# Idle products left out before the experts and before the recurrence; expert rows queued ahead of weights, early sums queued later

## The chip, the core and the metric

The kernel runs on one core of one Trainium2 chip. The metric is the device time of one execution in microseconds (us). TensorE is called PE here, VectorE DVE, ScalarE ACT, GpSimd POOL and SyncE SP. SP computes nothing; its queue issues most of the DMAs. All numbers in the text are in us unless another unit stands beside them.

## What is computed

Two transformer-like blocks follow each other on 1024 rows of 256 numbers. A layernorm stands behind each of the four parts.

```python
x = _layernorm(x + attention(x))            # 16 heads, causal, low-rank keys and values
x = _layernorm(x + experts64(x))            # 64 experts, 8 per row, room for 128 rows in each
x = _layernorm(x + recurrence(x))           # gated recurrence over the sequence and a gated branch
x = _layernorm(x + experts8(x))             # 8 experts, 2 per row, and a shared expert

# experts64
topw, topi = jax.lax.top_k(probs, 8); topw = topw / jnp.sum(topw, axis=-1, keepdims=True)
xe = jnp.zeros((64, 128, 256)).at[flat_e, pos].set(x_rep, mode='drop')
g, u = jnp.split(jnp.einsum('ech,ehf->ecf', xe, gate_up_proj), 2, axis=-1)
ye = jnp.einsum('eci,eih->ech', jax.nn.silu(g) * u, down_proj)
y = jnp.sum(y_flat.reshape(-1, 8, 256) * topw.reshape(-1, 8)[..., None], axis=1)

# recurrence
f = jnp.tanh(x @ w_f); g = jax.nn.sigmoid(x @ w_i) * jax.nn.silu(x @ w_v)
state = ft * state + gt                     # scan over the 1024 rows
out = jax.nn.silu((x @ w_q) * states) @ w_ro + ((x @ w_up) * jax.nn.silu(x @ w_gate)) @ w_down
```

## The kernel before, in words

Each engine has a program of its own, written out by hand. The order in the code is the order on the engine, and semaphores tie the engines together. The 1024 rows are 8 tiles of 128. Three stretches matter here.

**Tail of the routing.** Rows go to the experts through a buffer in memory, `xe_d`. POOL's `send` (L658) issues 8 indirect DMAs for each tile, one for each of a row's 8 choices. The choices are sorted, so that choice k of a row never goes to an expert below k. For the last tile this comes after the attention: `transpose_x1`, `route` and `count_places` on PE, the choosing on DVE, then the 8 sends. Behind `count_places` PE runs 40 products that nobody reads (`run_idle`, L1584), and 6 ahead of `transpose_x1`. SP loads the rows of experts two at a time (`load_rows`, L504), experts 0 and 1 when sends 0 and 1 of the last tile have landed, 2 and 3 behind sends 2 and 3, and so on to 7. Then SP issues `w_c` and `wo_c` (L524 and L525), 2 MB of weights of the recurrence, and only then the loop that loads rows and weights of experts 8 and up. The weights of experts 0 to 7 are loaded at the end of the attention.

**The 64 experts.** A ring of 8 buffers holds rows (`xe`) and weights (`gu_w`, `dn_w`). For each expert PE transposes the rows (`transpose_rows`, L1786, called T here), multiplies with the first weights (`gate_up`, L1797) and with the second (`down`, L1807). PE's order is T(e+2), gate_up(e+1), down(e). DVE copies, multiplies and works out where each row goes home to (`find_mine`, `find_home`), ACT does the silu and scales the result, and POOL sends 128 result rows home (`send_home`, L688). Experts 0 to 7 and 56 to 63 are written out; the 48 between them run as a hardware loop of 6 turns on PE, DVE and ACT. T(10) opens the first turn, and T(58) is the first behind the loop.

**The gap and the recurrence.** When all results are home, SP gathers the 8 results of each row (`load_results`, L536), the first four choices in one load, the others in a second. PE meanwhile runs 58 more unread products, in parts that wait for `moved` and `gath`. POOL adds choices 0 and 1 onto 2 and 3 (`sum_early`, L702). DVE adds the rest (`combine`, L1294), L1076 to L1080 take the variance, POOL makes `rstd` (L653), DVE normalises to `x2` (`finish_x2`, L1084), PE transposes (`transpose_x2`, L1830) and projects (`project`, L1840, in three parts). DVE's `middle` multiplies the gates (L1314), scans (L1317), and closes with L1320 and L1325. POOL's order within step t is `rstd` of tile t+1, `sum_early(t+2)`, `rstd` and normalising of tile t-1 (L708). DVE's order in step t is combine(t+1), the adding of the mix of t-1 (L1332), finish_x2(t+1), variance of the mix, middle(t). During this stage SP also loads 1 MB of `w1` for the last part with each tile (L516).

Of the kernel before, what the change touches and what calls it, by code (L numbers as in the profile page):

```python
# [7 lines left out]
T, HID = 1024, 256  # L8
TILES = T // P
# [22 lines left out]
KEY = T * E0  # L32
IDLE_START = 10
# [3 lines left out]
def build(nc, x, xT, wq, wq_ropeT, wkv_aT, kv_ln, wkv_b, woT, router0T, gate_up0, down0, w_in, init_state,  # L37
# [5 lines left out]
    with ctx:  # L43
# [116 lines left out]
        w_c = cutC2(6, HC, HID)  # L160
        wo_c = cutC2(2, HC, HID)
# [101 lines left out]
        sent_last = moved[1::2]  # L263
# [8 lines left out]
        gath_early = [sem(f"gath_early{u}") for u in range(2)]  # L272
        early_summed, sum_step = sem("early_summed"), sem("sum_step")
# [35 lines left out]
        def home_turn(e, u):  # L309

            return turn(e, u) + (32 if u % 2 else 0)
# [136 lines left out]
        def _(sp):  # L448
# [69 lines left out]

            for u in range(2):
# [29 lines left out]
            for t in range(TILES):  # L549
# [50 lines left out]
        def _(pool):  # L600
# [54 lines left out]
            def send(t, k):  # L655
# [3 lines left out]
                                        None).then_inc(sent[k % 2] if t < TILES - 1 else sent_last[k // 2], 16)  # L659
# [32 lines left out]
            for e in range(RING):  # L692
                send_home(e, e)
            with pool.Fori(1, E0 // RING) as i:
                for u in range(RING):
                    send_home(RING * i + u, u)
# [45 lines left out]
        def _(act):  # L742
# [93 lines left out]
            for e in range(RING):  # L836
                expert_act(e + 1, (e + 1) % RING)
                expert_out(e, e)
            with act.Fori(1, E0 // RING - 1) as i:
                for u in range(RING):  # L840
                    expert_act(RING * i + u + 1, (u + 1) % RING)
# [1219 lines left out]
```

## Time and profile before

| | us |
|---|---|
| three runs | 835.5, 831.17, 835.47 |
| their median | 835.47 |
| the profiled execution | 835.53 |
| its span in the trace | 833.7 |

The profiled execution is 1.8 longer than its span, which is what lies around the first and the last instruction. PE is busy for 94% of the span, DVE for 68%, ACT for 48% and POOL for 33%. The busy time of PE holds the unread products too. A row of a timeline reads: start, duration, engine, line, operation, output and inputs, count, and in brackets the idle time ahead of it with what ended it. Merged rows (x8 and the like) span from the first start to the last end.

### The profile page before, as it was taken

How to read it: one execution, taken by the hardware profiler on the slowest of the kernel's cores; microseconds unless marked ns; L12 is line 12 of the kernel's file. 1: busy time of each engine (PE TensorE's matmuls, PEld its weight loads, DVE VectorE, ACT ScalarE, POOL GpSimd, SP SyncE). 2: the span in 40 equal slices, each digit the busy share in tenths (PEclk: the TensorE clock that was granted, in tenths of full speed). 3: DMA queues.
4: the chain of work that ended last, by engine and by line, in shares of the span. 5: the costliest groups of instructions: out<-in, count | busy, mean ns of one | idle time of the engine just before them, and what ended most of it. 6: DMA issues, size and time to landing. Idle time of an engine off the chain costs nothing.

```text
span 833.7 us, 16672 instructions
## 1 busy us (share of the span) xinstructions
PE 780.8 (94%) x4645; PEld 662.9 (80%) x4645; DVE 565.5 (68%) x1422; ACT 397.6 (48%) x898; POOL 272.0 (33%) x357
## 2 busy tenths in 40 slices
PE   7999989999999999999897999998889999999997
PEld 6888867778778777777697898897888778888786
DVE  5323778777877777777644677458857367777766
ACT  1325656655566666666323444312333256666531
POOL 2004445443343333230354565614422500000061
PEclk9998999999999999999998999999998999999999
DMA  7449961000000000000559999777720335555431
GB/s 210 105 104 370 405 238 41 28 28 28 28 21 28 21 18 24 14 28 15 167 157 342 355 357 360 260 254 251 304 102 20 107 112 151 153 151 151 120 94 65
DMA packets 63032, 120.63 MB, mean 145 GB/s; under 512 B 18304, under 2 KB 31616, under 8 KB 62848
## 3 DMA queue, kind: packets, MB, share of 16 engines
q1 hardware_dynamic: 51984, 95.41, 34.9%
q0 software_dynamic: 7680, 21.51, 7.2%
q10 hardware_dynamic: 3312, 3.02, 1.0%
q8 instruction: 29, 0.48, 0.2%
q14 instruction: 27, 0.22, 0.1%
HBM read 76.13 MB, written 43.78 MB: 144 GB/s over the span
## 4 chain that ended last, share of the span: by engine, by line
PE 69%; DVE 12%; issue 7%; ACT 4%; DMA 3%; POOL 3%; SPq 1%; DVEq 0%; ACTq 0%; POOLq 0%
PE scores L1578 9%; PE scores L1577 9%; PE scores L1576 9%; PE probsT_ps L1687 6%; PE scores L1797 5%; PE acc_ps L1987 5%; PE acc_ps L1714 4%; PE misc_ps L1702 4%; PE misc_ps L1700 3%; DVE xT_lo L1054 2%; PE misc_ps L1584 2%; DVE neg_max L1048 2%; PE scores L1807 2%; POOL xd_d L729 2%; PE scores L1840 2%
## 5 line engine op out<-in xcount | busy, mean ns | idle before, releaser
L778 ACT ACTIVATE area<-scores,neg_max 128x128 f32<-128x128 f32 (+7 forms) x128 | 94.9, 742 | 76.7 <-DVE neg_max L1048 75.7
L1048 DVE TENSOR_REDUCE neg_max<-scores 128x1 f32<-128x128 f32 (+7 forms) x128 | 95.7, 749 | 24.6 <-PE scores L1663 24.5
L1687 PE MATMUL probsT_ps<-ident,area 128*128 128x128 f32 x552 | 84.1, 277 | 12.9 <-DVE xT_lo L1054 12.0
L1054 DVE TENSOR_TENSOR xT_lo<-probsT_ps,xT_hi 128x512 fp32r<-128x512 f32 x92 | 62.9, 687 | 38.3 <-ACT xT_hi L785 36.7
L1687 PEld LDWEIGHTS probsT_ps<-ident,area 128*128 128x128 f32 x552 | 63.1, 143 | 24.9 <-issue 19.5
L658 POOL DMA_INDIRECT xe_d<-x_rows,send_i x64 | 64.1, 1001 | 55.8 <-ACT x_rows L802 38.8
L688 POOL DMA_INDIRECT ye_d<-area,home_i x64 | 61.4, 959 | 48.9 <-issue 23.0
L1797 PE MATMUL scores<-area 128*96 128x128 f32 x512 | 68.7, 278 | 1.1 <-DVE area L1220 0.6
L1576 PE MATMUL scores<-kT_hi,weff_hi 128*128 128x512 f32 (+3 forms) x172 | 67.1, 390 | 1.9 <-issue 1.3
L785 ACT ACTIVATE xT_hi<-probsT_ps 128x512 fp32r<-128x512 f32 x92 | 54.0, 594 | 25.1 <-PE probsT_ps L1687 24.8
L1797 PEld LDWEIGHTS scores<-area 128*96 128x96 f32 x512 | 60.5, 166 | 3.2 <-DVE area L1220 2.5
L1578 PE MATMUL scores<-kT_hi,weff_lo 128*128 128x512 f32 (+3 forms) x172 | 62.1, 361 | 0.0
L646 POOL CAST weff_hi<-area 128x256 fp32r<-128x256 f32 x42 | 17.0, 406 | 137.8 <-PE scores L1663 90.2
L1577 PE MATMUL scores<-kT_lo,weff_hi 128*128 128x512 f32 (+3 forms) x172 | 62.0, 360 | 0.0
L1714 PE MATMUL acc_ps<-area,sgd 128*128 128x256 f32 x196 | 60.2, 389 | 1.6 <-DVE x_rows L1071 1.2
L735 POOL DMA_INDIRECT area<-yd_d,slot x16 | 15.8, 984 | 137.4 <-DMA yd_d<-area 132.8
L1702 PE MATMUL misc_ps<-xT_lo,xT_hi 128*128 128x512 f32 x144 | 57.8, 402 | 0.7 <-DVE xT_lo L1054 0.6
L1700 PE MATMUL misc_ps<-xT_hi 128*128 128x512 f32 x96 | 47.7, 497 | 0.0
L1576 PE MATMUL scores<-xT_hi,weff_hi 128*128 128x512 f32 x110 | 46.0, 419 | 0.0
L826 ACT ACTIVATE area<-scores 96x128 f32<-96x128 f32 x64 | 17.5, 273 | 57.1 <-PE scores L1797 57.1
L1987 PE MATMUL acc_ps<-area 128*128 128x256 f32 x184 | 43.5, 379 | 0.8 <-DVE area L1462 0.8
L1071 DVE SCALAR_TENSOR_TENSOR x_rows<-acc_ps,rinv,x_rows 128x256 f32<-128x256 f32 x90 | 42.3, 470 | 2.2 <-PE acc_ps L1714 2.2
(258 smaller groups left out, 1944.5 us busy)
## 6 DMA issues: line engine op xcount, KB each, us to landing
area<-gate_up SPq DMA_DIRECT2D x32, 384.0 KB
area<-w SPq DMA_DIRECT2D x23, 512.0 KB, 3.9
xe_d<-area SPq DMA_DIRECT2D x8, 1088.0 KB, 11.3
area<-xe_d SPq DMA_DIRECT2D x32, 272.0 KB, 6.2
ye_d<-area SPq DMA_DIRECT2D x8, 1024.0 KB, 16.7
area<-ye_d SPq DMA_DIRECT2D x16, 512.0 KB, 4.9
area<-w SPq DMA_DIRECT2D x8, 1024.0 KB, 7.3
area<-down SPq DMA_DIRECT2D x32, 192.0 KB
```

The lines of the kernel that those rows point to most:

```text
L778: act.activation(row_of(n)[:, 0:L], score_bank(n)[:, 0:L], ACT.Exp, bias=neg_max[:, n % 4:n % 4 + 1], accum_out=rsum[:, s, k:k + 1]).then_ ...
L1048: dve.tensor_reduce(neg_max[:, n % 4:n % 4 + 1], score_bank(n)[:, 0:(n // HEADS + 1) * P], AX.X, ALU.max, negate=True).then_inc(max_ready, 1)
L1054: dve.tensor_tensor(pT_lo[b % 3], seat_of("block", b)[:], pT_hi[b % 3].bitcast(f32), ALU.subtract).then_inc(lo_done, 1)
L1576: pe.matmul(out_ap, lh, rh, start=start, stop=False)
L1577: pe.matmul(out_ap, lh, rl, start=False, stop=False)
L1578: return pe.matmul(out_ap, ll, rh, start=False, stop=stop)
L1687: last = pe.transpose(seat_of("block", b)[:, i * P:(i + 1) * P], row_of(QUAD * G + i)[:, k * P:(k + 1) * P], ident[:])
L1700: pe.matmul(ctx_ps[:], latent[:, k, :], pT_hi[b % 3], start=k == 0, stop=False)
L1702: pe.matmul(ctx_ps[:], latent[:, k, :], pT_lo[b % 3], start=False, stop=k == tile_of(G)).then_inc(ctx_step, 1)
L1714: pe.matmul(out_of(n), ctxT[:, G % 2, i * P:(i + 1) * P], wvo[:, h * HID:(h + 1) * HID], start=True, stop=True).then_inc(out_ready, 1)
L1797: last = pe.matmul(half[b][0:I0, part * P:(part + 1) * P], gu_w[:, u, c, part * I0:(part + 1) * I0], xeT[:, b, c, :], start=c == 0, stop=c ...
L1987: last = pe.matmul(acc[:, 0:HID], hdT[:, u, c * P:(c + 1) * P], w2_b[:, u, c, :], start=c == 0, stop=c == I1 // P - 1)
```

## The change

- PE's `run_idle` calls between the attention and the recurrence are gone: 6 and 40 products in the tail of the routing, 58 in the gap. The 10 at the very start stay.
- The weights of experts 0 to 15 (`IN_ADVANCE = 16`) are loaded in 8 DMAs into `area1`, which held the queries of the attention, as soon as POOL has split the last queries. `w_c` and `wo_c` follow them there.
- SP loads the rows of expert 0 behind send 0 and those of expert 1 behind send 1. Rows of experts 8 and 9 follow those of 6 and 7 directly. The ring of weights serves experts 16 and up.
- The first two experts' parts of `w1` now share their place with `w_c` and `wo_c`, so they are loaded after the recurrence.
- PE, DVE, ACT and POOL have the 64 experts written out; SP keeps its loop for experts 24 and up.
- POOL waits for `x2` of tile t+1 ahead of `sum_early(t+2)`.

```diff
+IN_ADVANCE = 16
-        sent_last = moved[1::2]
+        sent_last = moved[0:2] + [moved[k | 1] for k in range(2, TOP0)]
+        ld_first_row = sem("ld_first_row")
...
-                if past(e, RING):
+                if past(e, IN_ADVANCE + RING):
                     sp.wait_ge(ye_ps, e + 2 - RING)
...
-            sp.wait_ge(pT_ps, blocks_to(GROUPS))
-            for e in range(0, RING, 2):
-                load_weights(e, e)
-            sp.wait_ge(x1_done, TILES)
+            sp.wait_ge(q_split, TILES * PAIRS)
+            for e in range(0, IN_ADVANCE, 4):
+                sp.dma_start(first_gu[:, e:e + 4], gate_up0[:, e:e + 4]).then_inc(ld_first, 16)
+                sp.dma_start(first_dn[:, e:e + 4, :], down0[:, e:e + 4, :]).then_inc(ld_first, 16)
+            sp.dma_start(w_c, w_in).then_inc(ld_wc, 16)
+            sp.dma_start(wo_c, w_mix).then_inc(ld_wc, 16)
...
-            for e in range(0, RING, 2):
-                sp.wait_ge(sent_last[e // 2], 32)
+            for e in range(2):
+                sp.wait_ge(sent_last[e], 16)
+                sp.dma_start(xe[:, e:e + 1, :], xe_v[:, e:e + 1]).then_inc((ld_first_row, ld_xe[0])[e], 16)
+            for e in range(2, RING, 2):
+                sp.wait_ge(sent_last[e], 32)
                 load_rows(e, e)
-            sp.dma_start(w_c, w_in).then_inc(ld_wc, 16)
-            sp.dma_start(wo_c, w_mix).then_inc(ld_wc, 16)
-            with sp.Fori(1, E0 // RING) as i:
+            for e in range(RING, IN_ADVANCE + RING, 2):
+                load_rows(e, e % RING)
+                if e < 2 * RING:
+                    load_weights(IN_ADVANCE + e - RING, e % RING)
+            with sp.Fori(1 + IN_ADVANCE // RING, E0 // RING) as i:
...
-                load_w1(t)
+                if t + 2 < E1:
+                    load_w1(t + 2)
             sp.wait_ge(x3_done, TILES)
+            load_w1(0)
+            load_w1(1)
...
                 if before(t, TILES - 2):
+                    pool.wait_ge(x2_done, t + 2)
                     sum_early(t + 2, u)
...
-            for e in range(RING):
-                transpose_rows(e + 2, (e + 2) % RING)
-                gate_up(e + 1, (e + 1) % RING)
-                down(e, e)
-            with pe.Fori(1, E0 // RING - 1) as i:
...
-            for e in range(E0 - RING, E0):
+            for e in range(E0):
                 if e + 2 < E0:
                     transpose_rows(e + 2, (e + 2) % RING)
...
-            run_idle(8)
-            for u in range(RING - 4, RING):
-                pe.wait_ge(moved[u], home_turn(E0 - RING + u, u))
-                run_idle(5)
-            run_idle(10)
-            pe.wait_ge(gath[0], 16)
-            run_idle(20)
```

PE, from the last product of the routing (`count_places`) to the first expert, before:

```order
L1739 MATMUL scores<-chosen,earlier 128x64
L1584 MATMUL misc_ps<-ident 128x128 x14
L1584 MATMUL misc_ps<-ident 128x128 [waits last_sends,send_done]
L1584 MATMUL misc_ps<-ident 128x128 x5
L1584 MATMUL misc_ps<-ident 128x128 [waits last_sends]
L1584 MATMUL misc_ps<-ident 128x128 x19
L1786 MATMUL probsT_ps<-ident,area 128x128 [waits ld_xe0]
```

and in the changed kernel, where L1748 is `count_places` and L1791 is T:

```order
L1748 MATMUL scores<-chosen,earlier 128x64
L1791 MATMUL probsT_ps<-ident,area 128x128 [waits ld_first_row]
L1791 MATMUL probsT_ps<-ident,area 128x128
L1791 MATMUL probsT_ps<-ident,area 128x128 [waits ld_xe0]
L1791 MATMUL probsT_ps<-ident,area 128x128
L1802 MATMUL scores<-area 96x128 [waits ld_first,xeT_done]
```

The 40 unread products are gone, and T(0) waits for its own rows alone.

SP's queue, from the rows of experts 0 to 7 to those of expert 8 (the first L504 row behind the branch), before; `moved1`, `moved3`, `moved5` and `moved7` are the sends of the last tile in pairs:

```order
L504 DMA area<-xe_d 128x544 [waits moved1,sent0_1,sent0_0]
L504 DMA area<-xe_d 128x544 [waits moved3]
L504 DMA area<-xe_d 128x544 [waits moved5]
L504 DMA area<-xe_d 128x544 [waits moved7]
L524 DMA area<-w_in 128x3072
L525 DMA area<-w_mix 128x1024
L526 UNCONDITIONAL_BRANCH
L526 ISA
L504 ISA [waits home_done,xeT_ps]
L504 DMA area<-xe_d 128x544
```

and in the changed kernel, where L545 and L523 load rows and L515 and L516 weights, here of experts 16 and 17:

```order
L545 DMA area<-xe_d 128x272 [waits sent0_1,moved0,sent0_0,pT_ps]
L545 DMA area<-xe_d 128x272 [waits moved1]
L523 DMA area<-xe_d 128x544 [waits moved3]
L523 DMA area<-xe_d 128x544 [waits moved5]
L523 DMA area<-xe_d 128x544 [waits moved7]
L523 DMA area<-xe_d 128x544 [waits home_done,xeT_ps]
L515 DMA area<-gate_up 128x768
L516 DMA area<-down 96x512
```

The 2 MB of `w_in` and `w_mix` no longer stand between the rows of expert 7 and those of expert 8.

POOL in steps 0 and 1 of the recurrence, before (L653 is `rstd`, L702 `sum_early`, L708 the normalising of the tile before):

```order
L653 TENSOR_TENSOR rstd<-mv,minus_half 128x1 [waits var_done] x2
L702 TENSOR_TENSOR area<-area 128x512 [waits gath_early0]
L653 TENSOR_TENSOR rstd<-mv,minus_half 128x1 [waits var_done]
L702 TENSOR_TENSOR area<-area 128x512 [waits gath_early1]
L653 TENSOR_TENSOR rstd<-mv,minus_half 128x1 [waits var_done]
L708 TENSOR_SCALAR x_rows<-y,mv,rstd 128x256 [waits rstd_done]
```

and in the changed kernel, where the three lines are L683, L729 and L735:

```order
L683 TENSOR_TENSOR rstd<-mv,minus_half 128x1 [waits var_done] x2
L729 TENSOR_TENSOR area<-area 128x512 [waits gath_early0,x2_done]
L683 TENSOR_TENSOR rstd<-mv,minus_half 128x1 [waits var_done]
L729 TENSOR_TENSOR area<-area 128x512 [waits gath_early1,x2_done]
L683 TENSOR_TENSOR rstd<-mv,minus_half 128x1 [waits var_done]
L735 TENSOR_SCALAR x_rows<-y,mv,rstd 128x256 [waits rstd_done]
```

Nothing changes places on POOL's queue; `sum_early` gets a second wait, and the `rstd` and the normalising behind it wait with it.

## Rows read from the trace of the kernel before

**Rows 1.** Chain of waits, 360 to 640: start, duration, what.

```profile
428.58 3.50 DMA xe_d<-x_rows,send_i
434.81 9.35 DMA area<-xe_d
542.56 10.31 PE misc_ps L1584 x90
581.67 1.35 DVE area L1084
```

**Rows 2.** Timeline of PE: L1584 unread products, L1786 T of an expert.

```profile
417.91 10.80 PE L1584 MATMUL misc_ps<-ident 128*128 128x128 f32 x80
436.67 0.38 PE L1786 MATMUL probsT_ps<-ident,area 128*128 128x128 f32 x2
444.20 0.69 PE L1786 MATMUL probsT_ps<-ident,area 128*128 128x128 f32 x2 [4.31 <-DMA area<-xe_d]
449.64 0.38 PE L1786 MATMUL probsT_ps<-ident,area 128*128 128x128 f32 x2
525.40 0.38 PE L1786 MATMUL probsT_ps<-ident,area 128*128 128x128 f32 x2
533.10 0.38 PE L1786 MATMUL probsT_ps<-ident,area 128*128 128x128 f32 x2
```

**Rows 3.** Timelines of POOL and SP, and SP's line L504 alone.

```profile
419.64 1.04 POOL L658 DMA_INDIRECT xe_d<-x_rows,send_i  x1 [5.08 <-DVE send_i L1147]
423.50 8.91 SPq L504 DMA_DIRECT2D area<-xe_d  x4
432.46 1.45 SPq L524 DMA_DIRECT2D area<-w_in  x1
DMA to landing us min/median/max: 2.8/6.2/10.4
```

**Rows 4.** Busy time by stretch; behind POOL: granted clock, DMA share, GB/s.

```profile
418.00:419.00 1.00, 1.00 (x9) 1.00 (x8) 0.90 (x6) 0.65 (x3) 0.00 (x0) 0.65 0.01 1
...
421.00:422.00 1.00, 1.00 (x8) 1.00 (x8) 0.00 (x0) 0.00 (x0) 0.95 (x1) 0.65 0.37 139
...
442.00:443.00 1.00, 0.00 (x0) 0.00 (x0) 0.00 (x0) 0.00 (x0) 0.28 (x1) 0.59 1.05 418
...
449.00:450.00 1.00, 1.00 (x9) 0.90 (x9) 0.29 (x2) 0.43 (x2) 0.80 (x1) 0.99 1.09 378
...
480.00:500.00 20.00, 19.86 (x155) 18.18 (x154) 14.36 (x64) 9.47 (x26) 12.27 (x13) 1.00 1.05 358
```

**Rows 5.** The page's DMA issues: count, KB each.

```profile
area<-gate_up SPq DMA_DIRECT2D x32, 384.0 KB
...
area<-down SPq DMA_DIRECT2D x32, 192.0 KB
```

**Rows 6.** Timelines of DVE and PE at the start of the recurrence.

```profile
551.22 0.41 DVE L1084 TENSOR_SCALAR area<-area,mv,rstd 128x256 f32<-128x256 f32 x1 [0.68 <-POOL rstd L653]
...
552.71 0.38 PE L1830 MATMUL misc_ps<-ident,area 128*128 128x128 f32 x2
553.56 3.84 PE L1840 MATMUL scores<-area 128*128 128x128 f32 x32 [0.46 <-ACT area L849]
```

**Rows 7.** Timelines of POOL and DVE in step 4, then at 23.

```profile
581.60 1.27 POOL L702 TENSOR_TENSOR area<-area 128x512 f32<-128x512 f32 x1
...
583.83 0.43 DVE L1314 SCALAR_TENSOR_TENSOR area<-area 128x256 f32<-128x256 f32 x1
583.95 0.71 POOL L653 TENSOR_TENSOR rstd<-mv,minus_half 128x1 f32<-128x1 f32 x1 [1.08 <-DVE mv L1080]
584.29 1.00 DVE L1317 TENSOR_TENSOR_SCAN area<-area 128x128 f32<-128x128 f32 x2
585.75 0.42 DVE L1325 TENSOR_TENSOR area<-area,probsT_ps 128x256 f32<-128x256 f32 x1
...
23.16 0.74 POOL L648 TENSOR_TENSOR q_lo<-area,q_hi 128x256 fp32r<-128x256 f32 x1
23.26 0.92 DVE L1006 TENSOR_TENSOR weff_lo<-area,weff_hi 128x256 fp32r<-128x256 f32 x1
```

More of the change, by code:

```diff
@@ L309, in home_turn, with weights_of, await_weights @@
         def home_turn(e, u):
-            return turn(e, u) + (32 if u % 2 else 0)
+            return turn(e, u) + (16 if u < 2 else 32 if u % 2 else 0)
+        def weights_of(e):
+            if e < IN_ADVANCE:
+                return first_gu[:, e], first_dn[:, e, :]
+            return gu_w[:, e % RING], dn_w[:, e % RING, :]
+        def await_weights(eng, e):
+            if e < IN_ADVANCE:
+                eng.wait_ge(ld_first, 8 * IN_ADVANCE)
+            else:
+                eng.wait_ge(ld_gu[e % RING // 2], 2 * turn(e - IN_ADVANCE, e % RING))
         def steps_two(eng, body):
@@ L691, in _ @@
             pool.wait_ge(zeroed, 16 * ZEROINGS)
-            for e in range(RING):
[L693 to L696, printed above, removed]
+            for e in range(E0):
+                send_home(e, e % RING)
             def sum_early(t, u):
@@ L835, in _ @@
             expert_act(0, 0)
[L836 to L841, printed above, removed]
-                    expert_out(RING * i + u, u)
-            for e in range(E0 - RING, E0):
+            for e in range(E0):
                 if e + 1 < E0:
@@ L1228, in find_mine @@
             def find_mine(e, u):
+                if isinstance(e, int) and e == 0:
+                    dve.wait_ge(ld_first_row, 16)
                 dve.wait_ge(ld_xe[u // 2], turn(e, u))
@@ L1260, in _ @@
             gated(0, 0)
-            for e in range(RING):
-                copy_xeT(e + 2, (e + 2) % RING)
-                gated(e + 1, (e + 1) % RING)
-                if e % 2 == 0:
-                    find_mine(e + 2, (e + 2) % RING)
-                else:
-                    find_home(e + 1, (e + 1) % RING)
-            with dve.Fori(1, E0 // RING - 1) as i:
-                for u in range(RING):
-                    copy_xeT(RING * i + u + 2, (u + 2) % RING)
-                    gated(RING * i + u + 1, (u + 1) % RING)
-                    if u % 2 == 0:
-                        find_mine(RING * i + u + 2, (u + 2) % RING)
-                    else:
-                        find_home(RING * i + u + 1, (u + 1) % RING)
-            for e in range(E0 - RING, E0):
+            for e in range(E0):
                 if e + 2 < E0:
@@ L1772, in _ @@
             count_places(TILES - 1)
-            run_idle(14)
-            pe.wait_ge(send_done, TILES)
-            for j in range(2):
-                pe.wait_ge(last_sends, j + 1)
-                run_idle(6)
-            run_idle(14)
             def transpose_rows(e, u):
-                pe.wait_ge(ld_xe[u // 2], turn(e, u))
+                if isinstance(e, int) and e == 0:
+                    pe.wait_ge(ld_first_row, 16)
+                else:
+                    pe.wait_ge(ld_xe[u // 2], turn(e, u))
                 if past(e, 2):
@@ L1797, in gate_up @@
                         last = pe.matmul(half[b][0:I0, part * P:(part + 1) * P],
-                                         gu_w[:, u, c, part * I0:(part + 1) * I0], xeT[:, b, c, :],
+                                         weights_of(e)[0][:, c, part * I0:(part + 1) * I0], xeT[:, b, c, :],
                                          start=c == 0, stop=c == HC - 1)
@@ L1806, in down @@
                     pe.wait_ge(ye_done, e - 1)
-                pe.matmul(half[2 + b][:, 0:HID], hT[:, b, :], dn_w[:, u, :], start=True, stop=True).then_inc(ye_ps, 1)
+                pe.matmul(half[2 + b][:, 0:HID], hT[:, b, :], weights_of(e)[1], start=True, stop=True).then_inc(ye_ps, 1)
             transpose_rows(0, 0)
@@ L1811, in _ @@
             gate_up(0, 0)
[L1812 to L1821 removed]
+            for e in range(E0):
                 if e + 2 < E0:
```

20 lines of the change are left out of this document (9 added, 11 removed).

## The prediction, made before the changed kernel ran

> **What bounds the kernel now.** I read the chain of waits first, then the timelines of PE, POOL and SP around its long pieces, and last the granted clock by stretches of one us. The chain crosses three places that the change touches [rows 1]: sends and loads of rows with no work in them, unread products just ahead of the recurrence, and a DVE instruction in each step of the recurrence that takes 1.35 where its like takes 0.41 [rows 6].
>
> In the tail of the routing the unread products run from 417.91 to 428.71 [rows 2]. They cost little by themselves: the last tile's first send starts at 419.64, SP loads the first rows at 423.50 [rows 3], and PE could have started some 3 earlier, but would soon have waited, since the last pair of rows is issued only when send 7 has landed, at 428.58 + 3.50 = 432.1 [rows 1]. The loss is later. T(8) starts at 444.20 after 4.31 of waiting for its rows [rows 2], because those stand behind 2 MB of weights on SP's queue [rows 3]. In that wait the granted clock falls (a mean of 0.59 over 442 to 443, so at 442.4 if it goes from full to half at once) and it is back only at 449.0 [rows 4]. Half is 1.2 GHz, full 2.4. T(10) comes at 449.64 instead of about 443.
>
> From T(10) to T(58) the experts take (525.40 - 449.64)/48 = 1.578 each, and in the written-out part from T(58) to T(63) (533.10 - 525.40)/5 = 1.540 [rows 2]. PE sets both paces; it is busy for 19.86 of 20 [rows 4].
>
> In the recurrence DVE sets the step. POOL's early sum starts at 581.60 and ends at 582.87; DVE's L1084 starts at 581.67 and ends at 583.02 [rows 1, 7]. It stands still while POOL works, and PE waits for what it writes.
>
> **The change part by part**, against the profiled execution's own 835.53, which is 0.06 from the median of the three runs; I treat the two as one.
>
> *Tail, up to T(6).* Sends land 2.5 to 3.5 after their issue: for sends 0 and 1, about 423.50 - 420.99, since sends start 1.27 apart from 419.64 [rows 3]. Send 0 has then landed at 422.2, and the least landing time of such a load is 2.8 [rows 3], so T(0) can start at 425.0 and T(1) at 426.3. The rows of 2 and 3 come at about 428.9, of 4 and 5 at 431.4, of 6 and 7 at 432.1 + 2.8 = 434.9. Without the unread products PE has been idle for 7 and starts at half clock, where an expert costs twice 1.525, or 3.05. (1.525 is 1.540 less the small gaps in it.) The clock comes back 3.4 to 4.8 after work begins: it was low from 418.35 to 421.65 while products ran back to back, and T(8) started at 444.20 and the clock rose at 449.0 [rows 2, 4]. With it back at 430 to 433.5, T(6) starts between 436.0 and 437.3; before, it is 436.67 [rows 2]. The three products of `route` and `count_places` may meet a low clock too, for 0 to 0.7. Earlier rows and colder products cancel: **+0.2**, between -0.7 and +1.3.
>
> *T(6) to T(10).* The rows of 8 and 9 now follow at once those of 6 and 7. Their ring places are free (T(1) and `find_home` of 0 are over by 428), so they are issued at 432.6 and land at about 436; T(8) needs them at 440. The early weights, 16 x 288 KB [rows 5] and 2 MB more, are 6.8 MB or 19 at 358 GB/s [rows 4]. They start when POOL has split the last queries, ahead of the last tile's attention, and are in before the last sends. If they were not, the sends would share the DMA engines with them, for a few tenths. Four experts at 1.54 are 6.2 instead of 449.64 - 436.67 = 12.97 [rows 2]: **-6.8**, between -6.8 and -4.3 (if only the wait goes and the clock still falls). What is late next is nothing on DMA: SP's rows of 10 and 11 want T(3), which is over before the rows of 8 have landed.
>
> *Experts written out.* 48 x (1.578 - 1.540) = **-1.8**. The cover is that PE gets its code and weights in time. Two experts' loads and results are 384 + 192 + 272 KB and 2 x 128 KB (the first two from [rows 5], the others from the shapes), 1,104 KB or 1,130,000 bytes; in 2 x 1.540 that is 367 GB/s, against 358 seen with the DMA engines full [rows 4]. If 358 were the ceiling, the loads would fall behind by 0.04 an expert, 1.6 in the 40 that load both rows and weights. A row load lands in 6.2 at the median, and is issued about 7 experts or 10.7 ahead of its use, so some 4 are in hand [rows 3] and PE would not notice. I take the whole, with 0 as the other end.
>
> *The gap.* `x2` of tile 0 is ready at 551.22 + 0.41 = 551.63, yet its transposes start at 552.71, behind the last unread products, which end at 552.87 [rows 1, 6]. That wait goes: -1.0. In exchange PE comes out of 14 idle at half clock. The work up to the end of parts 0 and 1 of `project` is 0.44 + 3.6, and DVE waits for it [rows 6]. With the clock back after 4.8, of which 0.5 is waiting for ACT, half of 4.3 is lost: +2.1. With 3.4 it is +1.4, and if all of it runs at half clock +4.0. Together **+1.1**, between +0.4 and +3.
>
> *Early sums behind x2.* L1084 goes from 1.35 to 0.41 in six tiles. The first is hidden behind PE's cold start, so 5 x 0.94 = 4.7 at most. But POOL's 1.27 now begins at the end of L1084. With X for that end, POOL works from X + 0.1 to X + 1.35, and DVE's L1314, a product of two SBUF tensors, starts at X + 0.8 (583.83 against 583.02) [rows 7]. What that costs is seen at 23: DVE's L1006, also with two SBUF inputs and 0.43 long by itself (its like is L1314 [rows 7]), starts 0.10 behind a POOL instruction that ends at 23.90 and ends itself at 24.18, 0.28 later [rows 7]. So L1314 ends at X + 1.63 instead of X + 1.24, a loss of 0.39, and L1294 behind it may lose 0.05 to POOL's later normalising. L1325 was ready on both sides, PE's and DVE's, so it moves with DVE. 0.94 - 0.44 = 0.5 in 5 steps: **-2.5**, between 0 and -4.7.
>
> The Trainium skill (SBUF — State Buffer, section "Who interferes with whom") says that a DVE instruction with two SBUF inputs contends with a GpSimd one that reads SBUF, and that whoever starts first blocks the other for its whole length. The rows at 23 agree. Taken to the letter it holds for the scans as well.
>
> *The rest.* `w1` parts 0 and 1 are loaded after the recurrence; 2 MB at 358 GB/s is 6, and their first reader stands behind the routing of the last part and half of its shared expert, which is the cover. If that cover were gone, they would cost up to those 6.
>
> The sum: 0.2 - 6.8 - 1.8 + 1.1 - 2.5 = -9.8. **835.5 - 9.8 = 825.7.**
>
> **The rivals.**
>
> *Cold start of the experts.* With gaps between the first rows the clock stays at half until T(6). Four experts from 428.9 at 3.05 put it at 441.1 instead of 436.9: +4.2, or 830. For it: PE has a hole ahead of each of the first loads. Against: once T(2) is in, half-clock work of 3.05 an expert is longer than the 2.5 between two sends that bring two, so PE has no holes. The Trainium skill (TensorE: Matmul & The Clock Gate, section "HAM oscillation — how this bites in real kernels") warns of waits for DMA between bursts of products, each of which begins at half clock again; it speaks against taking the unread products out.
>
> *POOL blocks the scans too.* The `rstd` and L708 of POOL now fall onto the scans; if each of these costs DVE another 0.5 a step, the recurrence gains nothing: 828.2. Against: a scan starts at 584.29 while POOL's `rstd` runs from 583.95 to 584.66, and the two scans take 1.00, or 0.5 each [rows 7]. This is what the letter of the page on SBUF would give.
>
> *No block at all.* L1314 is let through as the scans are: 5 x 0.44 more, 823.5. The rows at 23 are against it.
>
> *The change doesn't do what it says.* The rows of 8 are still late, say because T(3) and `find_home` hold back rows 10 and the weights of 16 stand in front of those. The wait of 4.3 comes back at T(10): 830, or 832.5 with the low clock. Against: 576 KB of weights are 1.6 on the queue, not the 6 of `w_in` and `w_mix`.
>
> *Slower: code.* The 48 experts written out make four engines fetch new code while the DMA engines are full. Over 62 experts 9.8 is eaten from 0.16 an expert on; at 0.4 it would be 850. For it: DMA share 1.05 [rows 4]. Against: T(58) to T(63) are written out and take 1.540.
>
> **How the numbers follow.** The forecast with its bounds 0.60; cold start 0.13; scans 0.10; no block 0.07; rows still late 0.05; code 0.05. The likeliest is 825.7. The terms' ends seldom meet: about 819 below and 832 above hold eight in ten, with the first four rivals inside or at the edge. Three runs of this kernel lie 4.3 apart, and about 0.5%, or 4.2, is what a measurement of it can tell from no change: 831.3 is the line. Code slower 0.04 (0.01 of it in between), and a tenth of the forecast and a third of cold start and late rows above 831.3 make 0.12 for the same; faster 0.83, slower 0.05.
>
> **What would show it.** T(8) without idle time ahead of it, and T(10) at about 443, confirm the second term. T(10) to T(58) in 74, not 75.8, confirms the third. The granted clock is half at about 425 and at 552 and full within 5 of it; if it is full at once, the costs in the first and fourth term are wrong. L1084 at 0.41 with L1314 at about 0.8 in five tiles, and steps of 8.3 instead of 8.8, confirm the last; L1314 at 0.43 means no block. A PE with idle time that nothing releases within the experts would mean code.

## The result, and the profile after

| | before | changed |
|---|---|---|
| median | 834.06 (6 runs, 831.17 to 835.5) | 827.66 (6 runs, 826.82 to 828.25) |
| the profiled execution | 835.53 | 828.25 |
| its span | 833.7 | 826.1 |
| ratio of the runs | | 0.9926, 95% interval 0.9906 to 0.9947 |

The changed kernel is faster by 6.4 in the medians and by 7.6 in the two spans. 825.7 was predicted, with 819 to 832 as the range. A second measurement, on a chip of the same level (below), gave 825.84 against 835.0, which is 9.2 less, and a ratio of 0.9896 (0.986 to 0.9931).

The two spans part as follows. T(n) is the transpose of expert n's rows; "last product" is the last product of the attention.

| stretch | before | changed | difference | predicted |
|---|---|---|---|---|
| start to last product of the attention | 412.41 | 411.37 | -1.04 | 0 |
| last product to T(6) | 24.26 | 26.33 | +2.07 | +0.2 |
| T(6) to T(10) | 12.97 | 6.11 | -6.86 | -6.8 |
| T(10) to T(63) | 83.46 | 84.40 | +0.94 | -1.8 |
| T(63) to the last `down` | 3.95 | 3.95 | 0 | |
| last `down` to x2 transposes of tile 1 | 20.18 | 20.28 | +0.10 | +1.1 |
| those to the end of the recurrence's products | 63.42 | 60.44 | -2.98 | -2.5 |
| the rest | 213.05 | 213.22 | +0.17 | 0 |

Nothing that the prediction speaks of lies in the first row. Three further profiles, taken later on one chip of the same level, reach that point at 412.19 (changed kernel), 411.03 and 412.73 (variants of it), and the kernel before at 413.78 there, so it varies by about as much as the row says.

Timeline of PE in the changed kernel (start, duration, line, operation, idle time ahead with what ended it): L1739 is `route`, L1748 `count_places`, L1791 T, L1802 `gate_up`, L1827 the x2 transposes, L1837 `project`. They answer to [rows 2] and [rows 6].

```profile
414.03 0.69 PE L1730 MATMUL probsT_ps<-ident,x_rows 128*128 128x128 f32 x2 [2.66 <-DVE x_rows L1106]
415.22 1.09 PE L1739 MATMUL probsT_ps<-router,x1T 128*128 128x64 f32 x4 [0.51 <-issue]
...
417.54 0.23 PE L1748 MATMUL scores<-chosen,earlier 128*128 128x64 bf16 x1
424.09 0.69 PE L1791 MATMUL probsT_ps<-ident,area 128*128 128x128 f32 x2 [6.31 <-DMA area<-xe_d]
425.37 0.69 PE L1791 MATMUL probsT_ps<-ident,area 128*128 128x128 f32 x2 [0.59 <-DMA area<-xe_d]
...
428.73 0.69 PE L1791 MATMUL probsT_ps<-ident,area 128*128 128x128 f32 x2 [0.97 <-DMA area<-xe_d]
...
437.70 0.38 PE L1791 MATMUL probsT_ps<-ident,area 128*128 128x128 f32 x2
...
440.76 0.38 PE L1791 MATMUL probsT_ps<-ident,area 128*128 128x128 f32 x2
...
443.81 0.38 PE L1791 MATMUL probsT_ps<-ident,area 128*128 128x128 f32 x2
...
521.92 1.09 PE L1802 MATMUL scores<-area 128*96 128x128 f32 x8 [0.85 <-DVE area L1242]
...
546.01 0.66 PE L1827 MATMUL misc_ps<-ident,area 128*128 128x128 f32 x2 [13.85 <-DVE area L1106]
547.13 5.47 PE L1837 MATMUL scores<-area 128*128 128x128 f32 x32 [0.46 <-ACT area L871]
552.44 0.38 PE L1827 MATMUL misc_ps<-ident,area 128*128 128x128 f32 x2
```

T(0) starts 4.5 earlier than before, yet T(6) starts 1.0 later, and 2.07 later behind the attention, which itself ended 1.04 earlier. T(8) at 440.76 has no idle time ahead of it; in [rows 2] it had 4.31. The 0.69 of a T is its length at half clock, 0.38 at full.

Busy time by stretch; behind POOL come granted clock, DMA share and GB/s. They answer to [rows 4].

```profile
433.00:434.00 1.00, 1.00 (x7) 1.00 (x6) 0.00 (x0) 0.00 (x0) 0.61 (x1) 0.50 0.99 368
434.00:435.00 1.00, 1.00 (x7) 0.83 (x7) 0.38 (x2) 0.42 (x2) 0.34 (x1) 0.74 0.97 337
435.00:436.00 1.00, 1.00 (x11) 0.97 (x10) 0.60 (x3) 0.38 (x2) 0.00 (x0) 1.00 0.58 201
...
550.00:551.00 1.00, 1.00 (x9) 1.00 (x8) 0.23 (x1) 0.15 (x1) 0.69 (x1) 0.71 1.08 397
480.00:500.00 20.00, 19.84 (x152) 17.84 (x151) 12.83 (x63) 9.55 (x26) 12.40 (x14) 1.00 1.05 352
500.00:520.00 20.00, 19.56 (x151) 17.63 (x150) 12.52 (x62) 9.12 (x25) 11.46 (x13) 1.00 1.05 346
```

The clock is half until about 434.5, which is 10.4 after T(0), and in the gap until about 550.6, 4.6 after the transposes. From 480 to 520 the DMA engines are full and move 346 to 352 GB/s.

DVE and POOL in one step of the recurrence: L1106 was L1084, L1323 was L1314, L1326 the scans, L729 `sum_early`, L683 `rstd`. They answer to [rows 1, 7].

```profile
575.86 0.41 DVE L1106 TENSOR_SCALAR area<-area,mv,rstd 128x256 f32<-128x256 f32 x1
577.09 0.82 DVE L1323 SCALAR_TENSOR_TENSOR area<-area 128x256 f32<-128x256 f32 x1
577.95 1.01 DVE L1326 TENSOR_TENSOR_SCAN area<-area 128x128 f32<-128x128 f32 x2
...
576.36 1.27 POOL L729 TENSOR_TENSOR area<-area 128x512 f32<-128x512 f32 x1 [0.53 <-DVE area L1106]
577.59 0.73 POOL L683 TENSOR_TENSOR rstd<-mv,minus_half 128x1 f32<-128x1 f32 x1
578.42 1.40 POOL L735 TENSOR_SCALAR x_rows<-y,mv,rstd 128x256 f32<-128x256 f32 x1
```

L1106 takes 0.41, not 1.35. L1323 now takes 0.82, not 0.43, and ends 0.28 behind the end of L729. The scans keep their 1.01 for two, the first beside `rstd` and the second (578.47 to 578.96) beside POOL's normalising, L735.

### The profile page after: what moved, and what is told of

The parts are those of the page before. It is cut to its first block, busy times and chain, and to the rows that moved or that the text cites. A ratio compares the mean times of both kernels' runs of the same rounds, so it can differ in the third digit from the quotient of the medians.

```text
span 826.1 us, 15756 instructions
## 1 busy us (share of the span) xinstructions
PE 758.8 (92%) x4437; PEld 639.4 (77%) x4437; DVE 557.2 (67%) x1422; ACT 397.1 (48%) x898; POOL 271.0 (33%) x357
## 4 chain that ended last, share of the span: by engine, by line
PE 69%; DVE 10%; issue 9%; POOL 5%; ACT 3%; DMA 3%; SPq 0%; DVEq 0%; ACTq 0%; POOLq 0%
PE scores L1585 8%; PE scores L1587 8%; PE scores L1586 8%; PE scores L1802 7%; PE probsT_ps L1696 6%; PE acc_ps L1976 5%; PE acc_ps L1723 4%; PE misc_ps L1711 4%; PE misc_ps L1709 3%; PE scores L1812 3%; DVE xT_lo L1076 2%; DVE neg_max L1070 2%; POOL xd_d L757 2%; PE probsT_ps L1791 2%; PE probsT_ps L1920 1%
## 5 line engine op out<-in xcount | busy, mean ns | idle before, releaser
L1802 PE MATMUL scores<-area 128*96 128x128 f32 x512 | 69.4, 280 | 1.6 <-DVE area L1242 0.8
L1802 PEld LDWEIGHTS scores<-area 128*96 128x96 f32 x512 | 61.6, 169 | 3.3 <-issue 2.0
```

The lines of the kernel that those rows point to most:

```text
L1802: last = pe.matmul(half[b][0:I0, part * P:(part + 1) * P], weights_of(e)[0][:, c, part * I0:(part + 1) * I0], xeT[:, b, c, :], start=c == ...
```

## The experiments

Twelve runs were made, on four chips of two levels: the kernel before takes 835 on chip 5, close to the 834.06 above, and 866 to 868 on chips 0, 14 and 11. Each ratio is to the kernel before on the same chip. A stands here for the level of 835 (the result above, whose chip has no number on record, and the four runs on chip 5), B for the other level: four runs on chip 0, three on chip 14 and one on chip 11. The changed kernel itself never ran on B, so what it gains there isn't shown; its variants came to ratios from 0.9896 to 1.0031.

### The two kernels once more

Unchanged, both on A.

> The changed kernel as it is, once more, as the partner of the three others. If the gain belongs to the kernel it is again 0.99 to 0.995 of the kernel before, whatever this chip's own level: T(6) to T(10) 6.1 us, and a recurrence step of 8.1. If part of it was a property of the chip of the first runs (there the experts from T(10) to T(63) took 84.4 us, paced by the weights' loads from about T(45)), that stretch is over 88 us here, with ScalarE starting its silu more than 2 us after TensorE's products were done, and the ratio nears 0.998.

> The kernel before as it is, for its trace beside the others. If ScalarE's late starts come with the unrolled experts, this trace has none and T(10) to T(63) is 83.5 us, as it was. If they come with this chip, they are here too, one in each turn of eight experts, and the stretch is 94 us or more.

The changed kernel: 825.84, ratio 0.9896 (0.986 to 0.9931). Its profiled run has T(6) 26.44 behind the last product, T(6) to T(10) 6.11, T(10) to T(63) 86.33, and steps of 8.1 in the recurrence. The kernel before: 834.42, with 24.25, 12.90, 83.56 and 8.7. In neither does ACT start late behind products that are done. Set against each other as in the table above, these two profiles give -1.59 in the first row, +2.19, -6.79, +2.77, 0, +1.41, -3.01 and, in the last row, +1.31. The profiled execution of the changed kernel took 831.05, the longest of its eight, against their median of 825.84; so this pair of spans differs by 3.7 only, where the medians differ by 9.2. The third term of the prediction is on the wrong side twice, by 0.94 and 2.77. A third profile with the same code for the experts (both fillers, below) took 83.14 there, 0.3 to 0.4 less than the kernel before.

### Do the loads pace the experts?

```diff
+                n = 8 if past(e, IN_ADVANCE + RING) else I0
-                sp.dma_start(dn_w[:, u:u + 2, :], down0[:, bass.ds(e, 2), :]).then_inc(ld_gu[u // 2], 16)
+                sp.dma_start(dn_w[0:n, u:u + 2, :], down0[0:n, bass.ds(e, 2), :]).then_inc(ld_gu[u // 2], 16)
```

The same kernel ran on B first and on A later.

> The changed kernel, but of the down weights of experts 24 and up only 8 of the 96 rows are loaded, so those experts' results are other than the reference's. The number of DMAs and all code are the same, the bytes of an expert fall from 565 to 475 thousand. Theory (DMA rate is the limit): T(10) to T(63) falls from 84.40 to 53 x 1.531 = 81.1, and no wait at second experts is left; the total falls by 3.3. Rival (code): the waits stay, 84.4.

> The changed kernel with 8 of 96 rows of the down weights of experts 24 to 63, so that these loads carry 396 KB a pair in the place of 576 KB; those experts' outputs are wrong. If the loads pace the experts behind T(43) (1.694 us an expert), the pace goes to 1.531 and T(43) to T(63) from 33.9 us to 30.6. If it is the unrolled code, nothing changes: 33 to 34.

On A it took 825.05 (one run, span 823.0), and T(43) to T(63) 30.56, which is 1.528 an expert, against 33.88 and 35.06 in the two runs of the changed kernel. T(10) to T(63) took 81.07. Busy time by stretch of this run:

```profile
465.00:500.00 35.00, 35.00 (x276) 32.65 (x275) 23.61 (x115) 16.94 (x46) 22.04 (x23) 1.00 0.95 316
500.00:525.00 25.00, 25.00 (x197) 23.27 (x196) 16.77 (x83) 12.32 (x34) 15.63 (x17) 1.00 0.85 279
```

PE has no idle time in 60 us. Written out, the experts run at 1.53 once the loads are lighter, with the same code and the same number of DMAs; so with the full loads the bytes set the pace of the last twenty. Two experts move 1,130,000 bytes, and at the 346 to 352 GB/s of the two stretches above that is 3.27 to 3.21, or 1.63 to 1.605 an expert. The 1.694 and 1.753 that were measured are more; the rest isn't accounted for.

On B the same kernel has a span of 854.6. Of the 31.6 more, 14.1 lie between T(10) and T(63) (95.14 against 81.07), 7.0 ahead of the last product of the attention and 11.0 behind the recurrence's products; the stretches between add up to -0.4. Timeline of PE and of ACT on B:

```profile
449.73 1.11 PE L1803 MATMUL scores<-area 128*96 128x128 f32 x8 [0.17 <-issue]
451.35 0.70 PE L1813 MATMUL scores<-area 96*128 96x256 f32 x2 [0.51 <-DVE area L1249]
...
447.85 0.47 ACT L862 ACTIVATE area<-scores,hw 128x256 f32<-128x256 f32 x1 [0.16 <-PE scores L1813]
450.70 0.27 ACT L855 ACTIVATE area<-scores 96x128 f32<-96x128 f32 x1 [2.38 <-remote]
```

ACT sits idle for 2.38, and what ended it was not one of the core's engines ("remote"), while the products it needs had ended at about 448.9. ACT is idle for over 2 at seven places in these experts on B, at none on A; four of the seven end with "remote", three are put down to PE's products. PE waits behind them as in the second row. The looped experts of the kernel before have such places on B too (the run with early `w_c` and `wo_c` below), so they don't come with written-out code.

### Loops instead of written-out code

Experts 16 to 55 as a hardware loop of 8 on PE, DVE and ACT, and 16 to 63 on POOL (the cut of PE):

```diff
-            for e in range(E0):
+            for e in range(2 * RING):
                 if e + 2 < E0:
                     transpose_rows(e + 2, (e + 2) % RING)
...
+            with pe.Fori(2, E0 // RING - 1) as i:
+                for u in range(RING):
+                    transpose_rows(RING * i + u + 2, (u + 2) % RING)
```

> The changed kernel with experts 16 to 55 in a hardware loop again on PE, DVE and ACT (16 to 63 on POOL). The changed kernel takes 1.531 an expert from T(10) to T(43), then 1.69 with PE waiting at each second expert's first products. Theory (the DMA engines are the limit from T(43) on): the looped form runs at 1.578 and never waits for weights, or waits less, so T(10) to T(63) takes 83.5 to 84.5 as against 84.40, and the total stays within 0.5 of the changed kernel. Rival (fetching of written-out code stalls PE): the waits are gone and nothing else is lost, T(10) to T(63) takes under 83.5 and no wait at second experts is left; total 1 or more faster.

On B: 860.89, ratio 0.992 (0.9894 to 0.9946). T(10) to T(63) took 97.51, against 94.99 to 95.70 in the three written-out kernels on the same chip, one of them with light loads (96.34 to 98.38 on the other two chips of B). Within the loop PE's waits come once a turn:

```profile
492.62 0.70 PE L1837 MATMUL scores<-area 96*128 96x256 f32 x2 [0.81 <-DVE area L1258]
...
506.88 0.70 PE L1837 MATMUL scores<-area 96*128 96x256 f32 x2 [0.80 <-DVE area L1258]
...
521.16 0.70 PE L1837 MATMUL scores<-area 96*128 96x256 f32 x2 [0.55 <-DVE area L1258]
```

They lie 14.27 apart, where eight experts at 1.53 are 12.2. On B a turn costs 2. On this chip the loop over 40 experts was 1.8 to 2.5 slower than written-out code, which has late starts at places of its own. That is the sign that the prediction gave to writing out, from one profile each; whether it is worth 0.04 an expert on A isn't settled: no run on A had the loop and light loads.

### The early weights spread over the experts

The same 16 experts' worth of early weights, but for the first two of every eight:

```diff
-            if e < IN_ADVANCE:
-                return first_gu[:, e], first_dn[:, e, :]
+            if e % RING < 2:
+                k = e // RING * 2 + e % RING
+                return first_gu[:, k], first_dn[:, k, :]
```

> The changed kernel with the 16 early experts chosen as the first two of each eight (0, 1, 8, 9, ...) instead of 0 to 15; the other six of each eight use the ring of weights, those of 2 to 7 loaded at the end of the attention. Bytes in all are the same, but the experts' stage asks for 491 thousand bytes an expert all along instead of 270 at first and 565 from expert 16 on, that is 321 GB/s at 1.531 instead of 369. Theory (DMA rate): no wait at second experts, T(10) to T(63) 81.1 as against 84.40, total 3.3 faster than the changed kernel, about 824.4. Rival (code fetching): waits stay, 827.7.

On B: 864.41, ratio 0.9995 (0.9964 to 1.0026), T(10) to T(63) 98.38 and T(43) to T(63) 37.91. The other variant on this chip, with the early weights as in the changed kernel (the early sums, below), took 98.02 and 38.83. Nothing was gained on B, where ACT starts late nine times among these experts; it was not tried on A.

### The weights of the recurrence out of the way, alone

The kernel before, with `w_c` and `wo_c` loaded early and nothing else:

```diff
+            sp.wait_ge(q_split, TILES * PAIRS)
+            sp.dma_start(w_c, w_in).then_inc(ld_wc, 16)
+            sp.dma_start(wo_c, w_mix).then_inc(ld_wc, 16)
...
-            sp.dma_start(w_c, w_in).then_inc(ld_wc, 16)
-            sp.dma_start(wo_c, w_mix).then_inc(ld_wc, 16)
```

> The kernel before with one part of the change: the recurrence's weights go to the queries' old place and are loaded when the last queries are split, the first two parts of w1 after the recurrence. Unread products, loops, pairs of rows and early sums are as before. Theory (the rows of expert 8 waited behind these 2 MB): T(6) to T(10) falls from 12.97 to 6.2, 6.8 faster than the kernel before, 827.3. Rival (rows and weights of 8 and up, loaded together, bring the wait back): T(8) or a later one waits 2 or more, 829 to 831.

On B: 865.11, ratio 1.0006 (0.9971 to 1.004). The wait did go: T(6) to T(10) took 6.11, as in the changed kernel. But T(0) to T(6) took 12.16, where the kernel before takes 8.12 on A, and T(10) to T(63) 99.6. Of these 4.04, 2.4 are idle time of PE ahead of the first `gate_up` (2.75, on A 0.37): T(1) had ended at 435.39, but DVE, idle for 11.75 until then, began its copy only at 437.66, and no engine of the core ended that ("remote"). The rest is work at half clock behind this hole, from 438.3 to 441.7. The kernel before has no trace on B, so where the 6.8 went in all is open: they may have been given back ahead of T(6) and in the loop, or have been smaller on B to begin with.

### The early sums

The changed kernel without the new wait of POOL:

```diff
                 if before(t, TILES - 2):
-                    pool.wait_ge(x2_done, t + 2)
                     sum_early(t + 2, u)
```

> The changed kernel without POOL's wait for x2 ahead of the early sums, so that they run beside the normalising as in the kernel before. In the changed kernel the normalising takes 0.41, L1323 0.82 to 0.86, and a step 8.10; in the kernel before 1.35, 0.43 and 8.73. Theory (the early sum blocks whichever DVE instruction it meets): the step is 8.7 again, 5 x 0.6 = 3 slower than the changed kernel, 830.7. Rival (the shorter step comes from elsewhere, as from a lighter load of DMA): the step stays near 8.1, 827.7.

On B: 867.36, ratio 1.0031 (1.0 to 1.0061). Timelines of DVE and POOL; L1105 is the normalising, L1322 the product:

```profile
589.49 1.34 DVE L1105 TENSOR_SCALAR area<-area,mv,rstd 128x256 f32<-128x256 f32 x1
591.64 0.42 DVE L1322 SCALAR_TENSOR_TENSOR area<-area 128x256 f32<-128x256 f32 x1
...
589.41 1.26 POOL L729 TENSOR_TENSOR area<-area 128x512 f32<-128x512 f32 x1
```

The 1.34 are back, the step is 8.72 again, and the recurrence takes 63.63 from the second transposes, against 60.44 with the wait. This stretch is the same on A and B: 60.42 to 60.65 in every profile with the wait, 63.42 to 63.63 in every one without it. The other variant on this chip (the early weights spread, 864.41) has the wait and is 2.95 faster in the medians, which is the recurrence's 3.2. Against the kernel before neither gains on this chip, while the variants on the other chips of B have ratios of 0.9896 to 0.9959; why is open.

### Unread products, in the tail and in the gap

As in the kernel before (46 in the tail; 58 in the gap), one part each:

```diff
             head_slots(pe_slot)
+            run_idle(6)
             transpose_x1(TILES - 1)
...
             count_places(TILES - 1)
+            run_idle(14)
...
+            run_idle(14)
```

> The changed kernel with the 6 and 40 unread products of the tail of the routing put back, nothing else. In the changed kernel T(0) starts at 424.09, 13.4 after the attention's last product (410.70), and the clock stays at half until 434.3; T(6) starts at 437.70. Theory (half clock costs the gain of early rows): the clock is full by 422, the products end near 428, T(6) comes 26.0 after the last attention product instead of 27.0 (it was 24.9 in the kernel before, from 411.74), so the kernel is 1 to 2 faster than the changed one, at about 826. Rival (rows bound the start, the clock does not): T(6) as in the changed kernel or later, since the products occupy PE until 428, time 827.7 or more.

> The changed kernel with the 58 unread products of the gap put back, nothing else. In the changed kernel the transposes of x2 of tile 0 start at 546.01 and those of tile 1 6.43 later, in the kernel before 4.52 later. Theory: with the products the second distance is 4.5 again (-1.9), while the first transposes start about 1.0 later, behind the last unread product; net 0.9 faster than the changed kernel. Rival: the products in the gap cost nothing and save nothing, 827.7.

On B the tail's filler gave 863.85, ratio 0.9959 (0.9938 to 0.998), and T(6) came 28.69 behind the last product, later than in any other run on B (25.1 to 28.4). The gap's filler gave 859.22, ratio 0.9896 (0.9866 to 0.9927), with the second x2 transposes 4.52 behind the first (6.60 and 6.67 with the tail's filler alone and with the loops, on the same chip, which have no filler there) and 19.71 behind the last `down` (20.14 and 20.46 there).

The late T(6) of the tail's filler is no price of the filler. T(0) and T(1) ended at 432.29, and then PE had to wait for DVE, which started late as ACT does on B (timelines of PE and DVE):

```profile
431.69 0.60 PE L1798 MATMUL probsT_ps<-ident,area 128*128 128x128 f32 x4
436.43 2.02 PE L1809 MATMUL scores<-area 128*96 128x128 f32 x8 [4.14 <-DVE area L1242]
...
435.94 0.76 DVE L1242 COPY area<-probsT_ps 128x256 f32<-128x256 f32 x2 [11.52 <-remote]
```

On A the same wait is 0.37. So only A can price the filler. Both at once, on A, with 14 and 38 in the tail:

```diff
+            run_idle(14)
             transpose_x1(TILES - 1)
...
+            run_idle(38)
```

> The changed kernel with unused products in the gap (58) and in the last tile's tail (14 in front of the transposes, 38 behind the count, meant to end where the first rows land). If the cold clock is worth what the trace says, the gap gives back 1.9 us (x2 transposes 4.5 apart, not 6.4) and the tail 0.5 to 1.3 us in T(0) to T(6) and 0.7 in the route: 0.996 of the changed kernel, about 2.5 us less, and the fastest of all. If the product stream holds back what it should help, T(0) comes 1 to 3 us later after the last attention product than in the changed kernel, and only the gap's 1.9 are left or less.

824.86, ratio 0.9885 (0.9829 to 0.9942), not told apart from the changed kernel's 825.84. Timeline of PE, where each unread product counts twice:

```profile
418.48 8.73 PE L1593 MATMUL misc_ps<-ident 128*128 128x128 f32 x76
427.04 0.60 PE L1793 MATMUL probsT_ps<-ident,area 128*128 128x128 f32 x4
...
538.43 10.31 PE L1593 MATMUL misc_ps<-ident 128*128 128x128 f32 x90 [2.08 <-DMA ye_d<-area,home_i]
548.59 0.38 PE L1829 MATMUL misc_ps<-ident,area 128*128 128x128 f32 x2
549.43 3.84 PE L1839 MATMUL scores<-area 128*128 128x128 f32 x32 [0.46 <-ACT area L871]
```

T(0) starts 14.31 behind the last product, 12.7 without the filler: 1.6 late. T(0) to T(6) takes 12.32, 13.61 without. So T(6) comes 26.63 behind the last product, where the changed kernel has 26.33. The hole behind T(1) is larger here: PE waits 2.32 for the rows of experts 2 and 3, which SP issued 15.60 behind the last product, and 14.46 in the changed kernel. In the gap the transposes start at 548.59, with `x2` ready at 547.78, and the second ones come 20.55 behind the last `down` (20.28 and 21.09 without). And the tail's clock falls all the same (busy time by stretch, columns as above):

```profile
430.00:432.00 2.00, 0.56 (x3) 0.56 (x4) 0.00 (x0) 0.00 (x0) 0.11 (x1) 0.90 0.93 366
432.00:434.00 2.00, 2.00 (x11) 1.91 (x10) 0.42 (x1) 0.24 (x1) 0.00 (x0) 0.50 0.23 37
```

Last, both fillers cut to end where the data arrive, against the run with both:

```diff
-            run_idle(38)
+            run_idle(29)
...
-            run_idle(20)
+            run_idle(8)
```

> The kernel with both fillers, cut so that each ends about where the data arrive: 29 products behind the count in place of 38, 8 behind the last gather in place of 20. In the last run the fillers kept the clock at full speed but ran over: T(0) came 14.3 us after the last attention product where the rows allow 12.7, and the x2 transposes 16.0 us after the last down product where 13.9 are enough. If that is all that the fillers cost, T(6) now comes 25.0 us after the last attention product (changed kernel 26.4, both fillers 26.6, kernel before 24.3) and the second x2 transposes 18.5 us after the last down product (20.3 to 21.1, 20.6, 19.7 to 20.2): 3.3 us less than the changed kernel, a ratio of 0.986 to the kernel before. If later stages take it back (the loads that pace the last twenty experts do not start earlier), only the gap's 1.9 us are left, 0.988. If a product stream delays whatever DMA or scatter runs beside it, the arrivals themselves come later again and the ratio stays at 0.9885 or more.

On B: 858.29, ratio 0.9901 (0.9865 to 0.9936), which is the number of the third expectation but not its reason: the rows of 2 and 3 were issued 14.07 behind the last product, no later than without filler. T(0) came 12.30 behind the last product, in time, but PE then waited for rows (1.04) and 2.44 more behind another late copy of DVE (idle 8.61, "remote"), the clock was half from 434 to 440.8, and T(6) came 26.63 behind the last product. In the gap `x2` itself came 15.1 behind the last `down` and the clock had dropped again. No version is shown to beat the changed kernel: on A the difference is below what the measurement can tell, and on B the changed kernel has no time.

## Why the prediction was right, and where it was not

**T(6) to T(10)**: right to 0.1. -6.86 measured, -6.8 predicted, 6.11 in the four profiles of A that have the change. The 2 MB ahead of the rows were the cause of the wait: with them alone taken away it is gone too. That this alone brings the gain was not shown, since that run fell on B and gained nothing in total.

**Tail up to T(6)**: the mechanism was right, the size was not. T(0), T(1) and T(2) were put at 425.0, 426.3 and 428.9 and came at 424.09, 425.37 and 428.73. The attention ended 1.04 earlier, so behind it T(0) came 0.1 later than said and T(2) 0.9 later. The step that failed is "the clock comes back 3.4 to 4.8 after work begins", read from a place where products ran back to back [rows 2, 4]. (The 3.4 are the length of the low stretch, from 418.3 to 421.7; from the first of those products, at 417.91, it is 3.8.) Here the first 5 us of work have holes of 0.59 and 0.97, and the clock came back 10.4 after T(0), 5.8 after T(2). That is +1.33 for the first experts, and the cold `route` and `count_places` took their 0.7 (they end 6.40 behind the last product, 5.66 in the kernel before). The rival "cold start" named the same cause with a price of +4.2 on top of the +0.2; 1.87 on top was measured, under half of it, since the clock was back ahead of T(6). The run with fillers adds that warmth at T(0) does not help much when a hole follows: the clock fell at 431.6, just behind a hole of 2.32. How it would fare with the smaller holes of the changed kernel is not shown. The kernel before, which started 4.5 later and found its rows there, reached T(6) first.

The section "HAM oscillation — how this bites in real kernels" of the Trainium skill (TensorE: Matmul & The Clock Gate) says that bursts of products with waits for DMA between them each start at the low clock. The trace agrees in kind: 2.07 us lost in the tail. In total it is outweighed, since the same change took out a wait of 4.31.

**Experts written out**: wrong. -1.8 predicted, +0.94 and +2.77 measured, and -0.3 to -0.4 with the fillers. The step that failed is "some 4 are in hand [rows 3] and PE would not notice". The prediction had worked out that 1.540 an expert asks for 367 GB/s where 358 were seen, and then let the reserve cover it. That reserve was counted for loads of rows, while PE's waits came ahead of `gate_up`, which needs weights. The engines gave 346 to 352 in the changed kernel. Up to T(43) the pace was 1.531 (1.554 in the second profile); then the reserve was gone and the last twenty took 1.694 each. The run with light loads shows it: 1.528 to the end. A wait for a weight load is named in PE's rows by what came last on an engine ("DVE area L1242" at 521.92, a copy that usually ends behind the start of such products), and only the experiment put a name to it. In the kernel before, 1,130,000 bytes in 2 x 1.578 are 358 GB/s, what [rows 4] show. That follows from the pace, whatever sets it; but the DMA engines were full there as well (share 1.05), so part of the 0.04 that the prediction gave to the loop may have been the loads'. No run parts the two.

The rival "code" named its sign, a PE with idle time that nothing releases. On A it did not come: 60 us without idle time in the run with light loads, which has all the code. On B the late starts of ACT and DVE are of that kind, and in the loop PE's waits come once a turn. That would fit code that arrives late, but no run shows it.

**The gap**: +1.1 predicted, +0.10 measured, just under its range; the second pair of runs gives +1.41 (21.09 against 19.68), inside it. The cold start cost 1.91 (x2 transposes 6.43 apart in place of 4.52), as said (+2.1). The wait that went was worth 0.93 (1.0 was said). The transposes now start 0.15 behind `x2`, not 1.08. And `x2` itself is ready 13.7 and 13.9 behind the last `down`, before it 14.6 and 14.2, for which the prediction had no term. The last send home lands a little faster too (3.67 and 3.84 behind its issue, against 4.34 and 3.82); with unread products in the gap of the new kernel it was 4.70 to 4.82. Whether the products hold the send back is open.

**Early sums behind x2**: right. -2.98 measured, -2.5 predicted. L1323 takes 0.80 to 0.86 and ends 0.28 behind POOL's sum, as it was worked out from the rows at 23 [rows 7]. Five steps shrink by 0.62 to 0.71 and not by 0.5, and the last one grows by 0.31, for which the prediction had no term. The Trainium skill (SBUF — State Buffer, section "Who interferes with whom") says that the first of a two-input DVE instruction and a GpSimd one shuts the other out. That holds for the product (0.43 alone, 0.82 here) and not for the scans, which take 1.01 for two beside POOL's `rstd` and normalising. L1106 reads one SBUF tile. The same section counts its kind, `tensor_scalar`, among those that can contend, and the trace agrees: it was held for 0.94 when it started 0.07 behind the sum [rows 1, 7].

**The rest**: 0 predicted, +0.17 measured, +1.31 in the second pair.

**The sum**: -9.8 predicted, -7.6 in the spans, -6.4 in the medians, -9.2 in the medians of the second measurement. The total was met by terms that were off in both directions, which is in part luck. The terms on the tail and on the experts were together 4.6 too good; the others were 0.5, 1.0 and 1.0 too cautious (the last one in the first row of the table, where no term stood) and 0.17 too good.

## What to carry to other kernels

A stage that starts as soon as its first data are there can be slower than one that starts late and finds all of it: with holes in its first work PE stayed at half clock here for 10.4. Before taking a faster pace for granted, divide the bytes of a turn by the rate that the trace shows with the DMA engines full; if the pace asks for more, the gain lasts only as long as the reserve. An instruction of a helper engine that runs beside the critical one should be put where a short instruction pays for it, and then all instructions near the new place need a look.

## What the runs showed of the hardware

- One and the same kernel takes 823.0 on one chip and 854.6 on another, with 14.1 of the 31.6 in the 64 experts and ACT idle there seven times for about 2.4, four of them ended by no engine of the core. What ends them is not shown. They are there with looped and with written-out experts. In three runs on B with unread products ahead of T(0), DVE too was late with the first copy behind them, by 2.0 to 3.7. The recurrence does not differ: 60.45 and 60.46.
- 38 unread products ahead of the first expert kept the clock at 1.00 up to 430 and it was 0.50 at 432 to 434 nevertheless, after a stretch in which PE was busy for 0.56 of 2.
- Full DMA engines (a share of 1.03 to 1.05) moved 346 to 361 GB/s over stretches of 20 to 30 us, in loads of 192 to 384 KB with scattered rows beside them.
- DVE's scans kept their length beside two different POOL instructions, while a product of two SBUF tensors and a `tensor_scalar` were held until POOL was done.
